# First attention: VectorE's bias additions to the near-diagonal scores, one maximum earlier in its order

## The chip, the cores and the metric

The kernel runs on 1 core of one Trainium2 chip. The time is the device time of one execution in microseconds (us), median over runs. The core's engines work from their own instruction queues and meet only at semaphores: PE (TensorE, matrix products; its weight loads are shown as PEld), DVE (VectorE), ACT (ScalarE), POOL (GpSimd) and SP (SyncE, here the issuer of most DMAs).

## The reference, cut to what matters

A sequence of 4096 tokens of 256 numbers goes through one layer of attention with 16 heads of 16 and a relative position bias, a layer norm, a two-layer feed-forward part with local attention, and a layer norm. The change is in the first attention alone:

```
scores = jnp.einsum('bhid,bhjd->bhij', qh, kh)
rel = jnp.clip(pos[None, :] - pos[:, None], -K, K) + K          # K = 64
bias_r = jnp.einsum('bhid,rd->bhir', qh, rel_pe)
bias = jnp.take_along_axis(bias_r, jnp.broadcast_to(rel[None, None], (b, h, l, l)), axis=-1)
attn = jax.nn.softmax(scores + bias, axis=-1)
out = jnp.einsum('bhij,bhjd->bhid', attn, vh)
```

The bias depends on the distance of key and query only within 64 positions. Further off it is constant on each side and is folded into the keys.

## The kernel before, in words

`attend` does the first attention. Its work is 128 **chunks** (16 heads times 8 blocks of 512 queries), numbered n. For one chunk there are:

- 32 **maxima** (`max_group` on PE, `bank_max` on DVE). PE multiplies 128 queries with 512 keys into one of three shared PSUM banks (L491, with bias windows added by L495 near the diagonal), and DVE reduces the bank to one maximum per query (L767). The row maximum over all keys comes from them (`find_max`, `cut_high`, `cut_low`, `max_to_rows`, `place_max`) and enters the scores as two more rows of the queries.
- 16 **pairs of scores** (`score` on PE, L517 and L520), two tiles of 128 keys by 512 queries each, in one of two PSUM buffers. Pairs 0, 1, 2 and 15 touch the diagonal: there DVE adds the near bias in place (`near_add`, L743: two additions in pairs 0 and 1, one in pairs 2 and 15).
- 16 **exponentials** on ACT (`exp_pair`, L644, one per pair, into one of four buffers). For pairs 0, 1, 2 and 15 ACT first waits for `near_added`. PE may write pair s only when the exponential of pair s-2 is done (the wait on `exp_done` in `score`).
- 8 **quads** of products with the values (`pv_quad`, L532, two pairs each), summed in `out_ps`. At the end ACT copies `out_ps` (L667), PE sums its quadrants (`sum_quadrants`, L552) and DVE divides by the sum (`finish`, L774 and L776).
- while there are later heads, the bias blocks of a later chunk (`make_bias`, L543, read by ACT at L635).

The orders are written out by hand. PE's `chunk` has 8 turns. A turn is one quad and four slots, and each slot holds one maximum; the first two slots of a turn hold one pair of scores each behind the maximum. The maxima run ahead of the scores: slot 0 of chunk n is maximum 16 of chunk n+1. The scores run two turns ahead of the quads. So the last two turns of chunk n hold, in PE's order: quad 6, max 24, pair 0, max 25, pair 1, max 26, max 27, quad 7, max 28, pair 2, max 29, pair 3, max 30, max 31, the sum of the quadrants; here and below a maximum is named by its slot, and the pairs 0 to 3 are those of chunk n+1. Pair 15 of chunk n stands behind max 21, in turn 5.

A bank of the three is used again every third use (`bank_free`): max 28 waits for DVE to have read max 25, max 29 for max 26, max 30 for 27, max 31 for 28, and the sum of the quadrants for max 29.

DVE's `chunk` goes through the 32 slots in order. `NEAR_SLOTS` says ahead of which slot's reduction a near addition stands: pairs 0, 1 and 2 of the next chunk ahead of slots 26, 27 and 30, and pair 15 ahead of slot 23.

The chunks 0 to 117 are a loop of 59 rounds with two chunks each. Chunks 118 and 119 follow (119 without `make_bias`), then 120 to 125 in a second loop, then 126 (no maxima) and 127 (no next chunk).

Of the kernel before, what the change touches and what calls it, by code (L numbers as in the profile page):

```python
# [233 lines left out]
def attend(nc, q_parts, k_parts, v_wide, rel_T, ident, part_sum, attn):  # L234
# [9 lines left out]
    LEAD = 16  # L244
    TOTAL = HEADS * CHUNKS
    SLOT_SCORES = ((0, 1), (2, 3), (), ())
    NEAR_SLOTS = (26, 27, 30, 23)
    ROWS_SLOT = 20
    MAX_GROUPS = TPC * (TILES // TPC)
    with ExitStack() as ctx:  # L250
# [438 lines left out]
        def _(dve):  # L689
# [43 lines left out]
            def near_add(n, s):  # L733
                h, c = place(n)

                spans = {0: [(0, 0, 192, 1, 64), (1, 64, 320, 2, 0)],
                         1: [(0, 192, 448, 3, 0), (1, 320, 512, 4, 0)],
                         2: [(0, 448, 512, 5, 0)],
                         PAIRS - 1: [(1, 0, 64, 0, 192)]}[s]
                dve.wait_ge(scores_ready, n * PAIRS + s + 1)  # L740
                for tile, a, b, slab, u in spans:
                    part = scores[s % 2][:, tile, a:b]
                    ins = dve.tensor_tensor(part, part,  # L743
                                            near_bias[:, bass.ds(h % 2, 1), bass.ds(c * TPC + slab, 1), u:u + b - a],
                                            ALU.add)
                ins.then_inc(near_added, 1)
# [32 lines left out]
            def chunk(n, par, ahead):  # L779
                for slot in range(MAX_GROUPS):  # L780
                    k = LEAD + slot
                    if slot == NEAR_SLOTS[3]:
                        near_add(n, PAIRS - 1)
                    if ahead and slot in NEAR_SLOTS[:3]:
                        near_add(n + 1, NEAR_SLOTS.index(slot))
                    if k < MAX_GROUPS and ahead >= 1:
# [982 lines left out]
def build(nc, ins, out):  # L1769

    q_parts = nc.dram_tensor("q_parts", [HEADS, 3 * D, N], BF16, kind="Internal").ap()
    k_parts = nc.dram_tensor("k_parts", [HEADS, 3 * D, 2 * N], BF16, kind="Internal").ap()
    v_wide = nc.dram_tensor("v_wide", [HEADS, P, 2 * TILES * VW], F32, kind="Internal").ap()
    first_norm = nc.dram_tensor("first_norm", [P, TILES, E], F32, kind="Internal").ap()
    with ExitStack() as ctx:
        project_heads(nc, ins["x_T"], ins["w_in_T"], ins["b_in"], ins["pe_edges"], q_parts, k_parts, v_wide)
        first_stored = ctx.enter_context(nc.semaphore("first_stored"))
        tokens = ctx.enter_context(nc.sbuf_tensor("tokens", [P, TILES, E], F32))
        attend(nc, q_parts, k_parts, v_wide, ins["rel_T"], ins["ident"], ins["part_sum"], tokens)
        join_heads(nc, ins["x"], ins["w_out_T"], ins["b_out"], ins["ident"], tokens, first_norm,  # L1780
                   first_stored)
        local_layers(nc, ins["w_qkv"], ins["qk_rows"], ins["w_o"], ins["ln_gb"], ins["w_1"], ins["b_1"],
                     ins["w_2"], ins["b_2"], ins["rotary"], ins["masks"], ins["ident"], tokens, first_norm,
                     first_stored, out)
# [54 lines left out]
```

## Time and profile before

| what | value |
|---|---|
| median of 3 runs | 5563.9 us (5562.22 to 5565.97) |
| time of the profiled execution | 5562.97 us |
| its span, first to last instruction | 5561.3 us |
| PE busy | 93% of the span |
| DVE busy | 75% |
| ACT busy | 56% |
| mean granted TensorE clock | 0.959 |

The first attention is the stretch from about 0.2 to 3.76 ms of the span. A matmul's end is modelled and matmuls overlap, so PE's share of busy time is not a share of its peak. In a timeline, instructions of the same line that follow each other are merged into one row: its second number runs from the first start to the last end, and x3 says that there are three. Idle time stands in brackets with what ended it.

### The profile page before, as it was taken

What the parts mean: (1) busy time and instruction counts of PE and PEld (TensorE: products, weight loads), DVE (VectorE), ACT (ScalarE), POOL (GpSimd) and SP (SyncE); (2) the same over time, 40 slices, a digit from 0 to 9 for tenths busy, and PEclk for the clock granted to TensorE, in tenths of its full rate; (3) what the DMA queues carried; (4) which work ended last, traced back from release to release, by engine and by line L of the source; (5) the groups of instructions that cost most, each with busy time, mean ns of one, the idle gap of its engine ahead of it and who ended that gap; (6) DMA issues with size and microseconds to landing.
All of it is one profiled execution on the core that took longest, in us unless ns stands there. A gap on an engine that the chain in (4) does not pass through costs nothing. (4 is left out here: it accounts for less than half of the span.)

```text
span 5561.3 us, 115505 instructions
## 1 busy us (share of the span) xinstructions
PE 5158.7 (93%) x34272; PEld 2723.7 (49%) x34272; DVE 4147.2 (75%) x8689; ACT 3111.0 (56%) x4539; POOL 997.2 (18%) x791
## 2 busy tenths in 40 slices
PE   8599999999999999999999999998599989899989
PEld 4233333333333333333333333334488867788866
DVE  6488888888888888888888888871477744677755
ACT  4266666666666666666666666671266532456521
POOL 0211111111111111111111111100233310233211
PEclk9599999999999999999999999995699999999999
DMA  6312212222122122121221211111200000000000
GB/s 202 78 48 54 54 49 55 51 52 56 48 55 53 49 54 54 49 54 48 54 54 48 54 49 49 51 41 33 95 1 0 0 17 0 17 0 0 0 38 23
DMA packets 199753, 248.33 MB, mean 45 GB/s; under 512 B 60718, under 2 KB 128628, under 8 KB 197876
## 3 DMA queue, kind: packets, MB, share of 16 engines
q1 hardware_dynamic: 194532, 226.77, 14.8%
q0 software_dynamic: 5136, 20.45, 2.0%
q8 instruction: 50, 0.82, 0.1%
q14 instruction: 35, 0.29, 0.0%
HBM read 210.73 MB, written 36.18 MB: 44 GB/s over the span
## 5 line engine op out<-in xcount | busy, mean ns | idle before, releaser
L767 DVE TENSOR_REDUCE group_max<-shared_ps 128x1 f32<-128x512 f32 x4096 | 2682.7, 687 | 581.9 <-PE shared_ps L491 476.5
L644 ACT ACTIVATE probs<-scores 128x1024 f32<-128x1024 f32 x2048 | 2012.0, 1021 | 1045.8 <-PE scores L517 667.5
L491 PE MATMUL shared_ps<-keys,max_queries 96*128 96x512 bf16 x4096 | 1434.2, 385 | 2.0 <-issue 1.7
L517 PE MATMUL scores<-queries,keys 98*128 98x512 bf16 (+3 forms) x4096 | 1214.3, 371 | 90.9 <-ACT probs L644 89.8
L532 PE MATMUL out_ps<-probs,values 128*17 128x512 f32 x8192 | 1083.1, 601 | 0.4 <-ACT probs L644 0.4
L491 PEld LDWEIGHTS shared_ps<-keys,max_queries 96*128 96x128 bf16 x4096 | 395.7, 97 | 1116.0 <-DVE group_max L767 506.9
L231 POOL TENSOR_TENSOR near_window<-near_bias,one_f 128x1536 bf16<-128x1536 f32 x128 | 351.4, 2746 | 2912.0 <-DVE max_parts L761 2263.2
L517 PEld LDWEIGHTS scores<-queries,keys 98*128 98x128 bf16 x4096 | 359.3, 98 | 466.5 <-ACT probs L644 241.1
L543 PE MATMUL shared_ps<-block_q,block_table 96*128 96x32 bf16 x4096 | 271.5, 233 | 81.1 <-POOL block_q L428 81.1
L543 PEld LDWEIGHTS shared_ps<-block_q,block_table 96*128 96x128 bf16 x4096 | 231.2, 114 | 187.4 <-issue 138.2
L1190 POOL TENSOR_TENSOR norm<-norm,layer_expo 128x16 f32<-128x16 f32 x64 | 186.2, 2910 | 704.6 <-DVE norm L1576 704.6
L1448 ACT ACTIVATE sim_prob<-sim_prob,shift,norm 128x256 f32<-128x256 f32 x512 | 299.4, 588 | 10.0 <-DVE shift L1646 10.0
L532 PEld LDWEIGHTS out_ps<-probs,values 128*17 128x17 f32 x8192 | 135.9, 95 | 248.2 <-issue 172.0
L495 PE MATMUL shared_ps<-ident_b,near_window 128*128 128x128 bf16 x1536 | 255.2, 220 | 0.0
L743 DVE TENSOR_TENSOR scores<-scores,near_bias 128x192 f32<-128x192 f32 (+2 forms) x768 | 232.8, 334 | 21.0 <-PE scores L517 16.9
L1296 PEld LDWEIGHTS bank<-v_kept,prob_T 128*128 128x128 f32 x2048 | 238.2, 192 | 7.5 <-issue 2.0
L1296 PE MATMUL bank<-v_kept,prob_T 128*128 128x64 f32 x2048 | 235.8, 273 | 1.2 <-DVE tokens L1608 1.2
L635 ACT ACTIVATE near_bias<-shared_ps 128x512 f32 (+1 forms) x256 | 152.8, 597 | 133.6 <-PE shared_ps L543 133.4
L1428 ACT ACTIVATE squares<-bank 128x512 f32<-128x512 f32 x128 | 76.5, 598 | 262.5 <-PE bank L1249 262.5
L495 PEld LDWEIGHTS shared_ps<-ident_b,near_window 128*128 128x128 bf16 x1536 | 151.4, 99 | 123.3 <-issue 2.2
L1503 ACT ACTIVATE gate<-quad,b 128x512 f32<-128x512 f32 x96 | 66.1, 688 | 236.4 <-PE quad L1370 236.4
L1641 DVE CUSTOM_DVE_ANT_0 sim_prob<-quad,mask 128x256 f32<-128x256 f32 x512 | 181.8, 420 | 16.1 <-issue 13.3
(194 smaller groups left out, 5832.7 us busy)
## 6 DMA issues: line engine op xcount, KB each, us to landing
keys<-k_parts SPq DMA_DIRECT2D x384, 96.0 KB, 2.1
values<-v_wide SPq DMA_DIRECT2D x128, 272.0 KB, 2.7
keys<-k_parts SPq DMA_DIRECT2D x384, 64.0 KB, 2.0
keys<-k_parts SPq DMA_DIRECT2D x128, 132.0 KB, 2.4
k_parts<-part SPq DMA_DIRECT2D x96, 128.0 KB
queries<-q_parts SPq DMA_DIRECT2D x768, 16.0 KB, 1.7
max_queries<-q_parts SPq DMA_DIRECT2D x768, 16.0 KB, 1.7
keys<-k_parts SPq DMA_DIRECT2D x384, 32.0 KB, 1.8
```

What stands on the lines that cost most here:

```text
L231: return pool.tensor_tensor(out, in_, ones[:].to_broadcast(list(in_.shape)), ALU.mult)
L491: mm = pe.matmul(bank, max_queries[par][:, t * P:(t + 1) * P], keys[par][0:ROWS, (t + TPC * g) * P:(t + TPC * (g + 1)) * P], start=True, s ...
L495: mm = pe.matmul(bank[:, pos * P:(pos + 1) * P], near_window[par][:, slab, u:u + P], ident_b[:], start=False, stop=i == len(near) - 1)
L517: mm = pe.matmul(out[:, 0:cut], keys[par][:, c * P:(c + 1) * P], queries[par][:, 0:cut], start=True, stop=True)
L532: mm = pe.matmul(out_ps[32 * i:32 * i + VW, :], values[par][:, 4 * q + i, :], probs[(2 * q + i // 2) % 4][:, i % 2, :], start=q == 0, stop ...
L543: mm = pe.matmul(shared("bias", half)[:, i * TILES:(i + 1) * TILES], block_table[par][:, BLOCK_U - 1 - u:BLOCK_U - 1 - u + P], block_q[par ...
L644: act.activation(probs[s % 4][:], scores[s % 2][:], ACT.Exp).then_inc(exp_done, 1)
L743: ins = dve.tensor_tensor(part, part, near_bias[:, bass.ds(h % 2, 1), bass.ds(c * TPC + slab, 1), u:u + b - a], ALU.add)
L767: dve.tensor_reduce(group_max[par][:, k:k + 1], bank, AX.X, ALU.max).then_inc(max_read, 1)
L1190: pool.tensor_tensor(norm[par][:], norm[par][:], expo[:, 0:2 * LHEADS].rearrange("p (h a) -> p h a", a=1), ALU.pow).then_inc(S.norm_ready, 1)
L1296: mm = pe.matmul(o_ps[:, j * LD:(j + 1) * LD], prob_T[:, 2 * j + c, :], v[:, h * LD:(h + 1) * LD], start=c == 0, stop=c == 1)
L1448: ins = act.activation(prob[:, h, :], sim[:, h, :], ACT.Exp, bias=shift[:, head:head + 1], scale=norm[par][:, head, :], accum_out=total[:, ...
```

## The change

It changes the four numbers that place the near additions in DVE's order, each by one. Pair 15 now stands ahead of slot 22, pair 0 of the next chunk ahead of 25, pair 1 ahead of 26 and pair 2 ahead of 29. No instruction is added or removed, and no other engine's order is touched.

```diff
@@ -244,7 +244,7 @@
     LEAD = 16
     TOTAL = HEADS * CHUNKS
     SLOT_SCORES = ((0, 1), (2, 3), (), ())
-    NEAR_SLOTS = (26, 27, 30, 23)
+    NEAR_SLOTS = (25, 26, 29, 22)
     ROWS_SLOT = 20
     MAX_GROUPS = TPC * (TILES // TPC)
     with ExitStack() as ctx:
```

The place where they are used, in DVE's `chunk`:

```
for slot in range(MAX_GROUPS):
    k = LEAD + slot
    if slot == NEAR_SLOTS[3]:
        near_add(n, PAIRS - 1)
    if ahead and slot in NEAR_SLOTS[:3]:
        near_add(n + 1, NEAR_SLOTS.index(slot))
    ...bank_max of this slot...
```

## Rows read from the trace of the kernel before

**Rows 1.** The page's first part: busy time, share of the span, instructions.

```profile
PE 5158.7 (93%) x34272; PEld 2723.7 (49%) x34272; DVE 4147.2 (75%) x8689; ACT 3111.0 (56%) x4539; POOL 997.2 (18%) x791
```

**Rows 2.** Waits, 700 to 3900 us: waiting line, released by, us in total, times, longest.

```profile
ACT probs L644 <- DVE scores L743: 321.4, 385, 1.9
...
PE scores L517 <- ACT probs L644: 78.1, 224, 0.6
```

**Rows 3.** One chunk's period in three stretches: busy us of each engine, clock, DMA.

```profile
2018.58:2024.13 5.55, 4.82 (x31) 1.58 (x28) 5.39 (x12) 3.46 (x4) 0.00 (x0) 1.00 0.42 110
2024.13:2026.22 2.09, 2.09 (x19) 1.19 (x17) 1.60 (x4) 1.94 (x2) 0.00 (x0) 1.00 0.21 40
2026.22:2046.07 19.85, 19.85 (x148) 7.86 (x144) 15.80 (x28) 12.54 (x15) 4.12 (x3) 1.00 0.11 32
```

**Rows 4.** Timeline of DVE, end of an even chunk: start, us, instruction, count, idle before.

```profile
2016.18 1.99 DVE L767 TENSOR_REDUCE group_max<-shared_ps 128x1 f32<-128x512 f32 x3 [0.57 <-PE shared_ps L491]
2018.09 0.22 DVE L743 TENSOR_TENSOR scores<-scores,near_bias 128x64 f32<-128x64 f32 x1
...
2019.00 1.35 DVE L767 TENSOR_REDUCE group_max<-shared_ps 128x1 f32<-128x512 f32 x2
2020.27 0.69 DVE L743 TENSOR_TENSOR scores<-scores,near_bias 128x192 f32<-128x192 f32 x2
...
2021.46 0.69 DVE L743 TENSOR_TENSOR scores<-scores,near_bias 128x256 f32<-128x256 f32 x2
2022.06 1.87 DVE L767 TENSOR_REDUCE group_max<-shared_ps 128x1 f32<-128x512 f32 x3
2023.85 0.22 DVE L743 TENSOR_TENSOR scores<-scores,near_bias 128x64 f32<-128x64 f32 x1
2024.33 1.29 DVE L767 TENSOR_REDUCE group_max<-shared_ps 128x1 f32<-128x512 f32 x2 [0.25 <-PE shared_ps L491]
```

**Rows 5.** Timeline of ACT, the same stretch.

```profile
2021.15 1.02 ACT L644 ACTIVATE probs<-scores 128x1024 f32<-128x1024 f32 x1 [1.65 <-DVE scores L743]
2022.38 1.02 ACT L644 ACTIVATE probs<-scores 128x1024 f32<-128x1024 f32 x1 [0.21 <-DVE scores L743]
```

**Rows 6.** Timeline of PE, the same stretch.

```profile
2018.58 0.39 PE L491 MATMUL shared_ps<-keys,max_queries 96*128 96x512 bf16 x1
...
2019.13 0.27 PE L520 MATMUL scores<-queries,keys 98*128 98x256 bf16 x1
...
2021.52 0.39 PE L491 MATMUL shared_ps<-keys,max_queries 96*128 96x512 bf16 x1
2022.23 0.60 PE L517 MATMUL scores<-queries,keys 98*128 98x512 bf16 x2 [0.33 <-ACT probs L644]
...
2023.46 0.60 PE L517 MATMUL scores<-queries,keys 98*128 98x512 bf16 x2 [0.41 <-ACT probs L644]
...
2024.34 0.96 PE L552 MATMUL shared_ps<-sum_sel,out_copy 128*128 128x17 f32 x8
2025.23 1.05 PE L532 MATMUL out_ps<-probs,values 128*17 128x512 f32 x8
```

**Rows 7.** Timeline of PE at the same places of the next, odd chunk.

```profile
2046.13 0.39 PE L491 MATMUL shared_ps<-keys,max_queries 96*128 96x512 bf16 x1
...
2052.72 1.05 PE L532 MATMUL out_ps<-probs,values 128*17 128x512 f32 x8
```

**Rows 8.** Timeline at the end of chunk 118: the sum waits for max 29.

```profile
3538.76 1.87 DVE L767 TENSOR_REDUCE group_max<-shared_ps 128x1 f32<-128x512 f32 x3
...
3540.69 1.02 PEld L552 LDWEIGHTS shared_ps<-sum_sel,out_copy 128*128 128x128 f32 x8 [0.18 <-DVE group_max L767]
...
3541.73 0.13 PEld L532 LDWEIGHTS out_ps<-probs,values 128*17 128x17 f32 x8
```

**Rows 9.** Timeline of PEld at the end of chunk 126: the sum starts on an idle PE.

```profile
3740.48 0.97 PEld L552 LDWEIGHTS shared_ps<-sum_sel,out_copy 128*128 128x128 f32 x8 [0.44 <-issue]
3741.48 0.13 PEld L532 LDWEIGHTS out_ps<-probs,values 128*17 128x17 f32 x8
```

## The prediction

> **What bounds the kernel now.** I began with the page: PE is busy for 93% of the span, DVE for 75%, ACT for 56% [rows 1]. So VectorE's work as such is not short of room, and a change of its order alone can only pay where PE waits for something that this order makes late. Next I read who waits for whom in the attention. ACT's exponentials wait 321.4 us in all for near additions, and PE's scores wait 78.1 us for exponentials [rows 2]. A chunk takes 27.49 us (the three stretches of rows 3), so some 111 chunks lie in that view: 2.9 us of the first wait and 0.70 us of the second for each chunk. Only the second holds up PE.
>
> Then where in the chunk. In the stretch from quad 0 onward to max 24, 19.85 us long, PE is busy all the time. From max 24 to max 31 it is busy 4.82 of 5.55 us, and DVE 5.39 [rows 3]. So a chunk is paced by PE except in its last two turns, where PE, ACT and DVE form a chain. The timelines show its links in an even chunk:
> - Max 24 starts on PE at 2018.58 [rows 6], and its reduction at 2019.00. Max 25's follows at 2019.66 (two reductions in 1.35 us, of 0.69 each). Near addition 0 comes only at 2020.27 [rows 4].
> - The exponential of pair 0 starts at 2021.15, after 1.65 us of idleness [rows 5]. It ends at 2022.17, and pair 2 of the scores starts at 2022.23, PE having waited 0.33 us [rows 6].
> - Near addition 1 at 2021.46, exponential 1 at 2022.38 to 2023.40 [rows 4, 5], pair 3 at 2023.46 after a wait of 0.41 us. Behind that everything on PE is back to back: max 30, max 31, the sum at 2024.34, quad 0 of the next chunk at 2025.23 [rows 6].
>
> I measure from the reduction of max 24, T: quad 0 comes at T + 6.23 in the even chunk. In the odd one max 24 is at 2046.13, so T is 2046.56 with the same lag, and quad 0 is at 2052.72 [rows 7], T + 6.16.
>
> **The change, part by part.** Nothing is added, so each edit is worth what it does to T + 6.23 and T + 6.16.
>
> *Pair 15 ahead of max 22.* Max 21's reduction starts at 2016.83 (three in 1.99 us, so 0.65 apart [rows 4]). Near addition 15 goes from 2018.09 to about 2017.43. It costs the reduction behind it 0.13 us (2018.09 to the reduction at 2018.22), but DVE waits for PE at max 24, so that is hidden. The cover is the 0.10 us between the end of max 23's reduction (2018.22 + 0.68) and 2019.00; the step was in front of it before as well. Exponential 15 comes up to 0.66 us earlier, which takes away a small wait of PE at pair 1. What comes next is bound elsewhere, so: nothing.
>
> *Pairs 0 and 1 ahead of max 25 and 26.* Both near additions start one reduction earlier: 0 at T + 0.61 instead of T + 1.27, 1 at T + 1.80 instead of T + 2.46 (one pair of additions with its reduction takes 2021.46 - 2020.27 = 1.19 [rows 4]). Pair 0's last matmul ends at 2019.40 by the model [rows 6] and is wanted at 2019.61, so this addition does not wait. Exponential 0 then ends at about T + 2.50, and PE reaches pair 2 only at about T + 2.7: the wait of 0.33 is gone. Exponential 1 starts at T + 1.80 + 0.92 (as 2021.46 to 2022.38) and ends at T + 3.74, so pair 3 starts at T + 3.80, not T + 4.46. If PE were all, the sum would start at T + 4.68 (0.88 behind pair 3, as 2023.46 to 2024.34) and quad 0 at T + 5.57.
>
> *Who is late next.* The sum waits until DVE has read max 29. DVE has no slack in this stretch: from T on it works without a break. A reduction costs 0.60 us from start to start when its data are there (three in 1.87 us with 0.68 for the last: 2 x 0.60 + 0.68), and two additions the same 0.60. In the new order [24], near 0, [25], near 1, [26], [27], [28], near 2, [29], the start of [29] is T + 0.61 + 6 x 0.598 + 0.13 = T + 4.33, and its end T + 5.01 (before: about T + 4.93, the end of the three at 2023.93). *The move of pair 2 ahead of max 29* is the 0.13 in this: it used to come behind.
>
> From that end to quad 0 the trace has two cases. When the sum waits behind max 31 still streaming, weight loads start 0.06 us after the reduction's end (3538.76 + 1.87 = 3540.63 to 3540.69) and quad 0 is at 3541.73, 1.10 behind it [rows 8]. When PE has run dry, from the first weight load to quad 0 it is 1.00 us [rows 9], so 1.06 with the release. Here max 31 has been issued by T + 4.5 and done by T + 4.7, so PE has run dry and I take 1.05: quad 0 at **T + 6.06**. The banks hold nothing else up: max 29 needs [26] at T + 3.08, just as PE gets there, and max 30 and 31 have what they need.
>
> The gain is 6.23 - 6.06 = 0.17 in even chunks and 6.16 - 6.06 = 0.10 in odd ones, 0.137 on average. In the loop: 118 x 0.137 = 16.2 us. Chunks 118 and 119 are already held by max 29 (3541.73 lies 1.10 behind it [rows 8]); they gain nothing or lose 0.03. The six behind gain some 0.1 each: 0.5 in sum. In all **16.7 us**. The profiled execution took 5562.97 us, which gives 5546.3; the median of the runs is 0.9 above it, so 5547.
>
> The bounds: with 1.10 instead of 1.05 behind max 29 it is 0.09 per chunk, 11 us; with [24] to near 0 at 0.66, as far as [24] stands from [25] now, 6 us less, so 5 to 11 us. With near 2's 0.13 hidden the gain is 16 us more, 33.
>
> The row says that the next VectorE instruction starts 0.60 us after one of 0.68: they overlap by 0.08 [rows 4]. The Trainium skill, in "VectorE: DVE Perf Modes", section "The DRAIN you can't avoid", says that the next one does not start until the pipe is empty. With links as long as the instructions themselves (9 terms: 0.69 + 0.69 + 0.68 + 0.69 + 3 x 0.68 + 0.22 + 0.68 = 5.69) max 29 would end at T + 5.69, and the change would cost 0.54 us a chunk, near 5631. The rows speak against that rule here: by it the before order would already be later than it is.
>
> **The rivals.**
> - *Larger gain:* max 29 does not hold the sum, and PE goes at T + 5.57: 0.62 a chunk, 78 us, 5486. For it: ACT's wait of 1.65 us looks as if it were the whole matter. Against it: DVE's 5.39 busy of 5.55 us. 4%.
> - *No change:* the bounds above add up (the release costs 1.10, near 0 starts at 0.66), gain 5 us, 5559. A small gain is easily lost in that way, since two waits of PE worth 0.74 us are swapped for one of about 0.4 us ahead of the sum. 17%.
> - *Slower:* DVE's chain to max 29 is now the path, and its links could cost 0.65 instead of 0.60 us, the distance at which reductions follow when each waits for its data (2016.18, three in 1.99). Seven links make 0.35: quad 0 at T + 6.41, 0.21 later than now, 27 us, 5590. It decides from 0.62 per link. Against it: in this stretch the scores and banks lie ready ahead of DVE. That the links are as long as the instructions is counted here too. 8%.
> - That the change does nothing is not possible by the code: `NEAR_SLOTS` is read only in DVE's order, and each index falls on a slot that exists.
>
> **How the numbers follow.** My forecast, a gain of 11 to 33 us, has 71%. Faster by over 0.2% (11.1 us, about what a measurement of this kernel can tell from no change) is that and the larger gain: 75%. Within 0.2%: 17%. Slower: 8%. The range leaves out the larger gain, the slower case and a part of the no-change case: 5534 to 5559.
>
> **What the changed profile would show.** The period alternates no more by 0.07 us and is about 27.38. ACT's wait for near additions falls by some 0.7 us a chunk (exponential 15's; the others move with the exponential before them). PE's waits on L517 for ACT fall to under half, only pair 3's is left. New: PEld L552 waits for DVE L767 in each chunk, some 0.4 us. DVE is idle ahead of max 30 no longer. If L552 shows no such wait, the gain is far larger; if DVE's reductions in that stretch are over 0.62 us apart, there is no gain. Stretches outside the last two turns should keep their 19.85 us.

## The result, and the profile after

The changed kernel takes **5617.86 us** (median of 5 runs, 5610.33 to 5619.61) against 5563.9: a ratio of 1.0093, 95% interval 1.0082 to 1.0105. It is 54 us slower, where 17 us less was forecast. The profiled execution took 5610.33 us, 47.4 more than the one of before; the account below is made between these two.

First the waits of 700 to 3900 us, as in [rows 2], with a new one in the last row (PEld L552 is the weight load of the sum of the quadrants):

```profile
ACT probs L644 <- DVE scores L743: 281.3, 380, 2.0
...
PE scores L517 <- ACT probs L644: 27.7, 114, 0.4
...
PEld shared_ps L552 <- DVE group_max L767: 70.3, 111, 0.6
```

PE's waits for exponentials fell from 78.1 to 27.7 us, and the sum now waits for max 29 in each of 111 chunks. That much was forecast. One chunk in the three stretches of [rows 3]:

```profile
2013.36:2018.91 5.55, 5.21 (x31) 1.65 (x27) 5.35 (x12) 3.26 (x5) 2.83 (x6) 1.00 1.02 175
2018.91:2021.10 2.19, 1.97 (x16) 1.10 (x16) 1.73 (x5) 1.70 (x2) 0.00 (x0) 1.00 0.86 109
2021.10:2041.03 19.93, 19.93 (x148) 7.88 (x145) 15.87 (x28) 13.20 (x15) 4.13 (x3) 1.00 0.18 46
```

The sum is 27.67 us, where the chunks before took 27.48 and 27.56 in turn. The long stretch is unchanged: the 0.08 us between 19.85 and 19.93 are where it is cut (before, it ends at 2046.07, 0.06 us ahead of max 24 at 2046.13 [rows 7], and it begins 0.99 us behind the start of quad 0, here 0.97). So the loss lies in the last two turns. The timeline of DVE there, which answers to [rows 4]:

```profile
2014.67 0.70 DVE L743 TENSOR_TENSOR scores<-scores,near_bias 128x192 f32<-128x192 f32 x2 [0.20 <-issue]
2015.28 0.68 DVE L767 TENSOR_REDUCE group_max<-shared_ps 128x1 f32<-128x512 f32 x1
2015.88 0.68 DVE L743 TENSOR_TENSOR scores<-scores,near_bias 128x256 f32<-128x256 f32 x2
2016.47 1.87 DVE L767 TENSOR_REDUCE group_max<-shared_ps 128x1 f32<-128x512 f32 x3
2018.27 0.22 DVE L743 TENSOR_TENSOR scores<-scores,near_bias 128x64 f32<-128x64 f32 x1
2018.40 1.87 DVE L767 TENSOR_REDUCE group_max<-shared_ps 128x1 f32<-128x512 f32 x3
```

and of PE, which answers to [rows 6]:

```profile
2013.36 0.39 PE L491 MATMUL shared_ps<-keys,max_queries 96*128 96x512 bf16 x1
...
2013.91 0.27 PE L520 MATMUL scores<-queries,keys 98*128 98x256 bf16 x1
...
2017.81 0.60 PE L517 MATMUL scores<-queries,keys 98*128 98x512 bf16 x2 [0.21 <-ACT probs L644]
2018.25 0.60 PE L491 MATMUL shared_ps<-keys,max_queries 96*128 96x512 bf16 x2
2019.13 1.07 PE L552 MATMUL shared_ps<-sum_sel,out_copy 128*128 128x17 f32 x8 [0.28 <-DVE group_max L767]
2020.13 1.05 PE L532 MATMUL out_ps<-probs,values 128*17 128x512 f32 x8
```

T, the reduction of max 24, is 2013.36 + 0.43 = 2013.79. Near 0 starts at T + 0.89, not T + 0.61. From there all links have the lengths of the forecast: to near 1 1.21 us (2015.88 - 2014.67), to near 2 2.39, then 0.13, and max 29's reduction ends at 2018.40 + 0.68 = 2019.08, T + 5.29 instead of 5.01. Quad 0 is 1.05 behind it, at T + 6.34. So one link is late, by 0.28 us. "Issue" in the first row says that the profile shows nothing for which DVE itself waited; a wait in its sequencer does not stand in such a row.

**What the 0.20 us of "issue" are.** The view of line L743 alone shows also the register instructions of DVE's sequencer (DVEq) that work out the address of a near addition. Its columns: count, shortest, median and longest in ns, first and last start. Before, with near 0 at 2020.3:

```profile
L743 DVEq FUSED_REGOPS  x5: 151/157/216, 2019.8 to 2021.0; - x5
```

and after, with near 0 at 2014.7:

```profile
L743 DVEq FUSED_REGOPS  x4: 151/157/212, 2014.2 to 2015.1; - x4
```

Before, the first of them starts 0.1 us behind the reduction of max 25 (2019.66), and two of them (0.22 and 0.16 us) are done while that reduction runs. After, the first starts at 2014.23, 0.44 us behind T, which is 0.3 us behind the start of pair 0's last matmul (2013.91): when the scores arrive. Only then do the same two run, and near 0 follows. The wait for the scores stands in front of the address work, and that work has no cover any more. The Trainium skill, in "Perfetto Trace Analysis", section "Per-engine timelines", draws it so: an instruction of the sequencer alone waits for its semaphores in the sequencer, and only then is it executed; the trace agrees (2014.2).

**The rest is TensorE's clock.** 0.15 us more per chunk (27.67 less the mean of 27.52) is 19 us in 126 chunks, not 47. The record of the granted clock shows the other part: from 290 us to the end of the attention it falls to half speed 5 times before and 23 times after. One such fall, in stretches of the changed kernel (the columns as in [rows 3]; the clock is the third from the right):

```profile
2047.00:2048.20 1.20, 1.20 (x12) 0.91 (x15) 1.10 (x3) 1.20 (x2) 0.00 (x0) 1.00 0.22 45
2048.20:2051.60 3.40, 3.40 (x14) 0.89 (x7) 1.30 (x3) 0.83 (x2) 0.00 (x0) 0.50 0.24 68
2051.60:2055.00 3.40, 3.40 (x31) 1.63 (x30) 2.01 (x4) 1.91 (x3) 0.00 (x0) 0.99 0.00 0
```

In the middle one the clock is at its lower level, 1.2 GHz, and PE gets through 14 matmuls, not 31. The chunk with the fall lasts from max 24 at 2041.03 to max 24 at 2070.18, 29.15 us, and the one in front of it, from 2013.36, 27.67: a fall costs 1.48 us here. (From sum to sum, the 22 chunks of the loop that hold a fall take 29.22 us on average, 1.55 more than the plain ones.) Every fall, before and after, comes as quad 0 starts (T + 6.15 to 6.30 before, T + 6.42 to 6.77 after), right behind the stretch in which PE waits for exponentials and, after the change, ahead of the sum. 18 more falls at 1.5 us are 27 us; with the 19 that makes 46 of 47.4. That the falls and the late link belong together is so far only a count; experiments 1, 2, 7, 8 and 9 bear on it.

### The profile page after: what moved, and what is told of

Same layout as the page of the kernel before. It is cut to its first block and busy times, and to the rows that moved or that the text cites. A ratio compares the mean times of both kernels' runs of the same rounds, so it can differ in the third digit from the quotient of the medians.

```text
span 5608.6 us, 115505 instructions
## 1 busy us (share of the span) xinstructions
PE 5224.5 (93%) x34272; PEld 2731.1 (49%) x34272; DVE 4145.1 (74%) x8689; ACT 3111.8 (55%) x4539; POOL 997.1 (18%) x791
## 5 line engine op out<-in xcount | busy, mean ns | idle before, releaser
L532 PE MATMUL out_ps<-probs,values 128*17 128x512 f32 x8192 | 1094.6, 607 | 0.4 <-ACT probs L644 0.4
L743 DVE TENSOR_TENSOR scores<-scores,near_bias 128x192 f32<-128x192 f32 (+2 forms) x768 | 235.2, 337 | 54.1 <-issue 25.5
```

The source lines that it names most:

```text
L532: mm = pe.matmul(out_ps[32 * i:32 * i + VW, :], values[par][:, 4 * q + i, :], probs[(2 * q + i // 2) % 4][:, i % 2, :], start=q == 0, stop ...
L743: ins = dve.tensor_tensor(part, part, near_bias[:, bass.ds(h % 2, 1), bass.ds(c * TPC + slab, 1), u:u + b - a], ALU.add)
```

## The experiments

**1. The wait put on the addition itself.** The order of the change, but with the register work ahead of the wait (`near_bias[...]` stands for the whole index):

```diff
-                dve.wait_ge(scores_ready, n * PAIRS + s + 1)
+                ready = n * PAIRS + s + 1
+                ready = ready if isinstance(ready, int) else dve.to_reg(ready)
                 for tile, a, b, slab, u in spans:
                     part = scores[s % 2][:, tile, a:b]
                     ins = dve.tensor_tensor(part, part, near_bias[...], ALU.add)
+                    if tile == spans[0][0]:
+                        ins._wait_ge(scores_ready, ready)
```

> The changed order, with one more edit: the wait for the scores stands on the near addition itself, behind the register instructions that work out its address, instead of on the first of them. Theory R (the address work of near addition 0 runs only after the scores arrive, 0.28 us late in each chunk, and holds max 29 and the sum): near 0 starts 0.61 us after max 24's reduction instead of 0.89, quad 0 at T + 6.06 instead of 6.34, a plain chunk lasts 27.38 us instead of 27.67, and the TensorE clock falls about as seldom as before (5 times in the attention, not 23). About 5546. Rival N (near 2 ahead of max 29 holds the sum): near 0 moves, but the time stays over 5590. Rival C (the clock falls more often for a cause of its own, not through the longer chunk): chunks of 27.38 us, but again some 20 falls, 5575.

Measured: 5545.02 us (5542.82 to 5545.53), ratio to the kernel before 0.9960, interval 0.9946 to 0.9974. In one chunk T is 1980.01:

```profile
1980.01 0.69 DVE L770 TENSOR_REDUCE group_max<-shared_ps 128x1 f32<-128x512 f32 x1 [0.16 <-PE shared_ps L491]
1980.62 0.69 DVE L744 TENSOR_TENSOR scores<-scores,near_bias 128x192 f32<-128x192 f32 x2
...
1984.34 1.87 DVE L770 TENSOR_REDUCE group_max<-shared_ps 128x1 f32<-128x512 f32 x3
```

```profile
1985.07 1.06 PE L552 MATMUL shared_ps<-sum_sel,out_copy 128*128 128x17 f32 x8 [0.28 <-DVE group_max L770]
1986.06 1.77 PE L532 MATMUL out_ps<-probs,values 128*17 128x512 f32 x8
```

Near 0 at T + 0.61, max 29's reduction ends at 1985.02, T + 5.01, quad 0 at T + 6.05, a plain chunk 27.38 us, 5 falls of the clock. The place of a wait among DVE's instructions makes the difference of 73 us between this kernel and the changed one (the edit also puts the number waited for into a register, which shows as a register instruction of 0.04 us at this line; experiment 6 shows that this way of waiting gains nothing by itself). The late link of theory R is shown, and N falls. C's forecast for this kernel, some 20 falls, fails: without the late link the clock falls no oftener than before. Its thought, that the falls need not come through a longer chunk, is not refuted by this run; it comes back in experiments 2 and 7. This is also the kernel that the prediction described without knowing it: 5547 was its number. (The kernel before took 5566.27 on this chip, so the gain is 21 us, where 16.7 was forecast.)

**2. Pair 2 left ahead of slot 30:** `NEAR_SLOTS = (25, 26, 30, 22)`, with the wait as it was.

> The change without its move of pair 2: near additions ahead of slots 25, 26, 30 and 22. Theory R: near 0 still at T + 0.89, max 29's reduction ends at T + 5.16 (5.29 less 0.13), quad 0 at T + 6.22, where it is in the odd chunks before the change, so a plain chunk takes 27.54; with 5 to 10 falls of the clock 5567 to 5575. Rival N (the move of pair 2 is what costs): chunks no longer than before (27.52) and a time of 5564 or less. Rival C: chunks of 27.54 and again some 20 falls of the clock, 5595.

Measured: 5584.53 us (5582.72 to 5587.88), 1.0033 (1.0020 to 1.0045). Max 29's reduction ends at T + 5.16, quad 0 is at T + 6.21, the plain chunk 27.54: as theory R says. But the clock falls 17 times in this trace, more than the 5 to 10 that I gave it, and so the time is above R's range, about halfway to C's 5595. A plain chunk is 0.02 us longer than before (27.54 against 27.52), so the 12 additional falls do not come through the chunk's length. The 0.13 us of near 2 are real, and they are not what makes the change slow: without them near 0's lateness still eats the whole gain.

**3. Pair 0 alone:** `NEAR_SLOTS = (25, 27, 30, 23)`.

> Only pair 0's addition moved, to slot 25; pairs 1, 2 and 15 stay at 27, 30 and 23. Theory R: near 0 at T + 0.89, which pushes max 25 and 26 and with them near 1 back by 0.22 us, to T + 2.68. Exponential 1 and pair 3 follow, quad 0 at T + 6.45, a plain chunk 27.77, 32 us more in all and the falls of the clock on top: 5600 to 5640. Rival (the prediction's walk was right about near 0, at T + 0.61): near 1 at T + 2.40, quad 0 about where it was, 5556 to 5564.

Measured: 5633.31 us (5627.77 to 5643.29), 1.0118 (1.0101 to 1.0135). In one chunk max 24's reduction starts at 1968.01 and near 0 at 1968.90 with the same 0.20 of "issue"; near 1 is pushed to T + 2.69:

```profile
1968.90 0.70 DVE L743 TENSOR_TENSOR scores<-scores,near_bias 128x192 f32<-128x192 f32 x2 [0.20 <-issue]
...
1970.70 0.69 DVE L743 TENSOR_TENSOR scores<-scores,near_bias 128x256 f32<-128x256 f32 x2
```

```profile
1972.64 0.60 PE L517 MATMUL scores<-queries,keys 98*128 98x512 bf16 x2 [0.94 <-ACT probs L644]
...
1974.40 1.05 PE L532 MATMUL out_ps<-probs,values 128*17 128x512 f32 x8
```

Pair 3 then waits 0.94 us for exponential 1, against 0.41 in [rows 6], and quad 0 comes at T + 6.39 (6.47 in the other chunk of a round). The plain chunk is 27.75 on average, and the clock falls 35 times. The lateness of near 0 comes to the end over exponential 1 here: max 29 is read by 1973.17 (1971.30 + 1.87), before the sum starts at 1973.51.

**4. Pair 2 alone:** `NEAR_SLOTS = (26, 27, 29, 23)`.

> Only pair 2's addition moved, to slot 29; the others stay at 26, 27 and 23. Theory R: nothing waits for it; max 29's reduction ends at T + 5.06, PE comes to the sum at T + 5.27 to 5.34, as before. 5564, no change, 5 falls of the clock. Rival N: the 0.13 us it puts ahead of max 29 shows in each chunk, 16 us, 5580.

Measured: 5566.08 us (5561.62 to 5575.00), 1.0001 (0.9991 to 1.0010). Near 2 at T + 4.25, max 29 read by T + 5.06, quad 0 where it was. Its 0.13 us cost nothing as long as exponential 1 holds the sum. Of the three steps tried alone (this one, experiments 3 and 7) it is the only one that does nothing; pair 1 alone was not run.

**5. The wait on the addition, pair 2 ahead of slot 30:** experiments 1 and 2 together.

> The wait on the near addition itself as in the run wait_on_add, with pair 2's addition left ahead of slot 30 (25, 26, 30, 22). Theory R: with near 2 out of the chain to max 29, its reduction ends at T + 4.87 instead of 5.00 and quad 0 comes at T + 5.92; a plain chunk lasts 27.25, 16 us less over the attention, near 5529. Rival (PE or exponential 1 holds the sum next): the sum stays at T + 5.06 and the time at 5545.

Measured: **5522.59 us** (5521.31 to 5523.26), ratio to the kernel before 0.9924 (0.9907 to 0.9941). It beats both kernels. T is 1914.11 in this chunk:

```profile
1916.51 2.47 DVE L770 TENSOR_REDUCE group_max<-shared_ps 128x1 f32<-128x512 f32 x4
1918.90 0.22 DVE L744 TENSOR_TENSOR scores<-scores,near_bias 128x64 f32<-128x64 f32 x1
```

```profile
1919.04 1.06 PE L552 MATMUL shared_ps<-sum_sel,out_copy 128*128 128x17 f32 x8 [0.15 <-DVE group_max L770]
1920.03 1.05 PE L532 MATMUL out_ps<-probs,values 128*17 128x512 f32 x8
```

Max 29's reduction ends at 1918.98, T + 4.87, and quad 0 is at T + 5.92; a plain chunk takes 27.25 us. The clock does not fall once from 290 us to the end of the attention, and the five falls fewer than in experiment 1, some 7 us, account for the 6 us by which it is better than the 5529 expected.

**6. The control: the old order with the wait on the addition.**

> The order of before (26, 27, 30, 23) with the wait on the near addition itself: the control for the run wait_on_add. Theory R: in this order the scores have arrived long before near 0 and the address work is hidden either way, so near 0 stays at T + 1.26 and the plain chunks at 27.48 and 27.56: 5564 to 5566, no change. Rival (the way of waiting is worth something by itself, whatever the order): 5550 or less.

Measured: 5565.99 us (5559.90 to 5569.76), 1.0000 (0.9990 to 1.0010). Near 0 stays at T + 1.26. The way of waiting is worth nothing where the scores have long arrived.

**7. Pair 15 alone:** `NEAR_SLOTS = (26, 27, 30, 22)`.

> Only pair 15's addition moved, to slot 22; the others stay at 26, 27 and 30. Theory R: near 15 comes 0.45 to 0.6 us earlier, its register work shows here too, but DVE waits for max 24 behind it all the same: plain chunks stay at 27.48 and 27.56, 5564 to 5566. Rival: the 0.1 us of PE's wait at pair 1 that it removes shows as 5 to 10 us less, 5556.

Measured: 5580.36 us (5576.89 to 5592.25), 1.0028 (1.0018 to 1.0037). Both theories missed. The plain chunks are 27.48 and 27.56 as expected, and quad 0 stays at T + 6.16 and 6.23; but the clock falls 15 times. What did change is PE's wait ahead of pair 2:

```profile
1973.50 0.60 PE L517 MATMUL scores<-queries,keys 98*128 98x512 bf16 x2 [0.43 <-ACT probs L644]
```

It was 0.33 us [rows 6]. The small wait at pair 1 is gone, so PE comes 0.1 us earlier to the same late exponential 0. The idle time has moved, into the stretch behind which the clock falls. (The profiled execution took 5586.91 us, 24 more than that of before. Up to the last sum of the attention it is 16 us behind, 3773.4 against 3757.3, which is ten falls; the other 8 lie behind the attention.)

**8. Max 31's matmul three times,** in the changed kernel. The two extra ones write the same products into the same bank; they only keep PE busy:

```diff
+                for again in range(2 if k == LEAD - 1 else 0):
+                    pe.matmul(bank, max_queries[par][:, t * P:(t + 1) * P],
+                              keys[par][0:ROWS, (t + TPC * g) * P:(t + TPC * (g + 1)) * P],
+                              start=True, stop=True)
                 mm = pe.matmul(bank, ...
```

> The changed kernel, with the matmul of max 31 issued three times into the same bank instead of once, so that PE is busy for 0.43 us of what it idles ahead of the sum. Max 29 holds the sum as before, so quad 0 stays at T + 6.34 to 6.40 and the plain chunk at 27.67 to 27.73. If the falls of the clock come from PE's idle time ahead of the sum, they get rarer (from 23 to 5 or fewer) and the time goes to about 5585 to 5592. If they come with the chunk's length alone, they stay at 23 or more and the time at 5610 or over.

Measured: 5579.02 us (5576.36 to 5580.39), 1.0024 (1.0014 to 1.0034), below the 5585 to 5592 expected with rare falls. It is faster than the changed kernel by some 39 us, with two matmuls more in each chunk, 0.43 us from 1946.29 to 1946.72. The end of a chunk (lines are shifted by 4; L492 are the extra matmuls):

```profile
1946.29 0.59 PE L492 MATMUL shared_ps<-keys,max_queries 96*128 96x512 bf16 x2
1946.72 0.38 PE L495 MATMUL shared_ps<-keys,max_queries 96*128 96x512 bf16 x1
1946.95 1.07 PE L556 MATMUL shared_ps<-sum_sel,out_copy 128*128 128x17 f32 x8
1947.95 1.05 PE L536 MATMUL out_ps<-probs,values 128*17 128x512 f32 x8
```

Max 24 is at 1941.17 on PE, so T is 1941.60, and quad 0 comes at T + 6.35. The plain chunk stays at 27.67 us on average, and the clock does not fall once. So the chunk's length alone does not bring the falls; with PE's idle time ahead of the sum filled there are none.

**9. The same for experiment 7:** max 28's matmul three times, with pair 15 alone moved.

> The kernel of pair15_alone with the matmul of max 28 issued three times into the same bank, which fills 0.43 us of PE's idle time ahead of pair 2. The reduction of max 28 waits its turn on DVE and exponential 0 still sets pair 2, so the plain chunks stay at 27.48 and 27.56. If the 14 falls of the clock in pair15_alone come from the longer gap ahead of pair 2, they go, and the time is 5554 to 5560, which is also what the kernel before would take without its falls. If they come from something else that pair 15's move does, they stay at some 14 and the time at 5576 to 5592.

Measured: 5558.57 us (5556.18 to 5564.59), 0.9992 (0.9982 to 1.0001). The plain chunks are as in experiment 7, with one fall left, at 315 us, and pair 2 waits no longer:

```profile
1963.59 0.60 PE L492 MATMUL shared_ps<-keys,max_queries 96*128 96x512 bf16 x2
1964.03 0.38 PE L495 MATMUL shared_ps<-keys,max_queries 96*128 96x512 bf16 x1
1964.41 0.61 PE L521 MATMUL scores<-queries,keys 98*128 98x512 bf16 x2
```

With work that computes nothing new, the kernel is 22 us faster than that of experiment 7 (on another chip): the 15 us that moving pair 15 had cost are gone. Against the kernel before on its own chip (5563.62) it is 5 us faster, which its interval does not tell from none.

## Why the prediction was wrong

**The path: right.** PE paces all but the last two turns; max 29 would hold the sum once near 0 and near 1 came earlier; links of 0.60 us, 0.13 for near 2, 1.05 from max 29 to quad 0. These links are in the trace of the changed kernel, and with near 0 on time (experiment 1) the sum of the prediction comes out: T + 6.05 against 6.06, 27.38 us against 27.38, 5545.0 against 5547. The term for near 2, 0.13 us a chunk or 16 us, measured 0.13 between experiments 1 and 5 (T + 6.05 to 5.92), and 22.4 us with the five falls of the clock that went. The kernel before alternates between 27.56 and 27.48 us a chunk; the prediction's 27.49 is 0.06 short for the chunk it read, because its last stretch ends ahead of max 24, but its gain goes by T + 6.23 and 6.16 and does not use it.

**The step that failed** is this one: "Pair 0's last matmul ends at 2019.40 by the model and is wanted at 2019.61, so this addition does not wait." The arrival was right. But I took DVE to need the scores when the addition starts. Its sequencer needs them some 0.45 us earlier, at the first register instruction of the address, which carries the wait. I read DVE's own rows, where 0.60 from start to start hides that work, and never the rows of its sequencer at L743, which the same trace had: 2019.8, with 0.22 and 0.16 us in front of near 0. The upper bound for this link, 0.66, was taken from the spacing of reductions, which have one short register instruction each. It measured 0.89. With it the prediction's own sum gives T + 6.34 and 19 us slower.

**What was left out altogether** is the clock. The page gave 0.959, and I took it as given. The change of 0.15 us a chunk came with 18 more falls, 27 us, more than its direct cost. My case "slower" got the sign and a wrong mechanism: it priced links of 0.65 us at 27 us, where the late near 0 cost 19 by itself, and the links stayed at 0.60. So the sign that I had named, reductions over 0.62 us apart, did not show, and there was no gain all the same. That the 5631 for links as long as their instructions lies near the measured 5617.86 is chance: max 29 was read by T + 5.29, not T + 5.69.

**Pair 15 ahead of max 22, which the prediction put at "nothing",** was right for the chunk's length and wrong for the time: alone it costs some 15 us (5580.36 against 5565.56, the kernel before on the same chip), by 10 more falls of the clock in the trace. The reason that I gave, "What comes next is bound elsewhere", points to the likely cause: PE got to the place that bounds it 0.1 us earlier, and stood idle there longer. Experiment 9 shows that the falls need the idle time ahead of pair 2; that the 0.1 us more of it is what brings them is not shown apart from it. And in experiment 1 pair 15 was moved too, with no more falls than before, so it is not a cost of the move in every order.

**The new waits: right but for one.** PE's waits for ACT under half (78.1 to 27.7), the sum's wait on max 29 in each chunk (0.64 us by the weight loads, 0.28 by the matmuls), the two chunks of a round alike. ACT's wait for near additions fell by 40 us (321.4 to 281.3), 0.36 us a chunk, where 0.7 was forecast.

## What to carry to other kernels

The addition here takes its address from registers, and with the wait on the semaphore ahead of that register work it started 0.45 us later than the data were there. Moving such an instruction up to where its data have just arrived can expose that work. Read the sequencer's rows beside the engine's, and try the wait on the instruction itself. And ask of every edit where PE's idle time goes, not only how much of it there is: the same chunk length with 0.1 us of idle time in another place went with 15 us more here (experiment 7), and filling a gap with products that nobody needs won 39 back (experiment 8).

## What the runs showed of the hardware

- The register work between a wait and an addition with a computed address took 0.45 us from the first register instruction to the addition (2014.23 to 2014.67), two instructions of 0.21 and 0.16 us and the hand-over. Behind a reduction with its own wait, DVE's sequencer went on to register work only when that reduction had started: at 2019.68 behind 2019.66 before, at 2013.80 behind 2013.78 after, at 1980.03 behind 1980.01 in experiment 1.
- TensorE's granted clock fell to half (1.2 GHz) in the middle of a loop in which PE was idle for at most 0.4 us at a time (before and changed, 400 to 3500 us; 1.0 in experiment 3). These falls came between 0.3 us ahead of the start of quad 0 and 0.6 us behind it. Falls between 290 us and the end of the attention, by the plain chunk in us: 0 (27.25, experiment 5), 5 (27.38, experiment 1), 2 to 7 (27.52: 5 before, 7 in experiment 4, 2 in experiment 6), 15 (27.52, experiment 7), 17 (27.54, experiment 2), 23 (27.67, changed), 35 (27.75, experiment 3), and with the gap filled 0 (27.67, experiment 8) and 1 (27.52, experiment 9). In 8 and 9 the falls went with the gap. Which gap at which chunk length makes the clock fall stays open: experiment 1 had the same 0.28 us ahead of the sum as the changed kernel and 5 falls, experiment 5 had 0.15 there and none. The amount of idle time does not order them either: from 400 to 3500 us PE was idle for 78 us with 5 falls (before), 62 with 23 (changed) and 48 with 17 (experiment 2).
- The time of the kernel before varied from 5558.96 to 5574.83 us over 16 runs on one chip, that of the filled kernel of experiment 8 from 5576.36 to 5580.39 over 10 on another. The mean granted clock of the 16 goes with their times: 0.957 in the two slowest (5571.35 and 5574.83), 0.960 in two of the three fastest (5558.96 and 5562.25), 0.958 or 0.959 in all others. A varying number of falls in the attention would explain this in part; the stretch behind the attention varies too (1804 us from the last sum to the end in the profiled execution of the kernel before, 1812 in that of experiment 7). The falls were counted in one execution of each kernel, so which part is which stays open.
